# Cross-attention and an MX-FP8 feed-forward on one core: a new order of loads, a third place for queries and keys, two centerings on ScalarE

## The chip, the cores and the metric
One core of a Trainium2 chip runs the whole program in one launch. The metric is device microseconds of one execution; three executions of the kernel before gave 611.86 to 611.87 us, median 611.86. A profiled execution took 611.8 us by the same measure; its trace spans 610.0 us, so some 1.8 us lie around the trace.

## The reference
What is computed, cut to what matters (shapes: x 4x512x512, ctx 4x512x256, gate and up 2048x512, down 512x2048):

```python
x = x + xattn(layernorm(x), ctx, Wq, bq, Wk, bk)
x = x + ffn(layernorm(x), gate_w, up_w, down_w)

def xattn(logits, features, Wq, bq, Wk, bk):
    query = einsum('bnc,dc->bnd', features, Wq) + bq        # d = 128
    key = einsum('bnc,dc->bnd', features, Wk) + bk
    attention = softmax(einsum('bnd,bmd->bnm', query, key), axis=-1)
    return einsum('bln,bmn->blm', logits, attention)

def mx_dequant(t):     # blocks of 32 along the last dimension, e4m3
    scales = maximum(max_abs(blocks) / 448, 1e-30)
    return (blocks / scales).astype(float8_e4m3fn).astype(float32) * scales

def mx_linear(x, w):
    return mx_dequant(x) @ mx_dequant(w).T

def ffn(x, gate_w, up_w, down_w):
    h = silu(mx_linear(x, gate_w)) * mx_linear(x, up_w)
    return mx_linear(h, down_w)
```

## The kernel before
Everything stands in one function that writes an instruction list for each engine: SP (issues loads, stores and transposing DMAs), GpSimd (Pool: one reduction over partitions per weight unit, and accumulating DMAs), TensorE, ScalarE and VectorE. Each list is a row of calls of small helpers in an order written out by hand. An engine works its list strictly in order; between the lists stand only semaphores. So what sets the order around the change is these lists, and a table `bank_uses` that says, for each of the eight PSUM banks, which result uses it after which: a result waits until the one before it in its bank has been read (`take_bank`, `bank_left`).

Work is cut so:

- Attention, for each batch b of 4: `project(b, i)` makes the queries (i=0) and keys (i=1) from the context, `take_projection` copies them with the bias to SBUF; `energies(b, nt)` makes 128 rows of logits; `row_max` (VectorE), `exponential` (ScalarE) and `weigh` (ScalarE: identity times 1/sum) follow; `turn_probs(b, nt)` multiplies a piece of the exponentials by this diagonal, which turns and scales it; `take_probs` copies that to `AT`; `attend(b, lt)` multiplies the raw x columns by `AT`; `add_attended` (VectorE) adds it to the rows of x. These matmuls are float32. `row_means` and `row_variances` are the first layernorm's statistics on ScalarE.
- The 12 weight units (gate and up of four column groups, then four pieces of down), each 128x2048: load to one of three places `W`, then on VectorE `unit_reduce`, `unit_largest`, `unit_scale`, `unit_round`, `unit_dequant`, on ScalarE `unit_magnitude`, `unit_rescale`, then split into two float16 parts: `unit_hi` (ScalarE) writes the high part, an accumulating DMA of Pool (`unit_rest`) subtracts it from `W`, and `unit_lo` (ScalarE) writes what is left. SP turns each part with a transposing DMA (`turn_unit_hi`, `turn_unit_lo`).
- The rows of x after attention, batch by batch (`center`, `rows_scale`, `rows_round`, `rows_dequant`, `rows_hi`, `rows_rest`, `rows_lo`, `turn_rows_hi`, `turn_rows_lo`), the same way, into one of two places of `xT`. For batches named in `rows_by_vector` VectorE writes the low part without the DMA.
- `product(r, c)`: gate and up of 128 rows r (0 to 15) and 512 columns c: 24 matmuls of 512 columns in float16 (high by high, high by low, low by high). `silu_of` (ScalarE) and `hidden_of` (VectorE) make 128x512 of the hidden layer; a row's four pieces are quantized (`hidden_scale`, `hidden_round`, `hidden_dequant`), split (`hidden_hi`, `hidden_lo`) and turned into one of two places `hT`. The split's buffer has one place for each part: `hidden_lo(r)` waits until the low part of row r-1 has been turned, and `hidden_hi(r)` until `hidden_lo(r-1)` has read the high part. `turn_hidden_hi(r)` waits until `down(r-2)` is done.
- `down(r)`: 48 matmuls of 512 columns. `down_last` does row 15 in two halves of 48 matmuls of 256 columns; it starts when both parts of row 15 have been turned.
- TensorE begins with 18 matmuls of zeros (`keep_zeros`).

In the trace each line is that of a helper: L664 `project`, L671 `energies`, L678 `turn_probs`, L687 `attend`, L703 `product`, L715 and L718 `down`, L734 `down_last`, L748 `keep_zeros`, L929 `take_projection`, L970 `take_probs`, L1575 `hidden_lo` on VectorE, L1054 `hidden_hi`, L417 and L422 the turning of a hidden row's high and low part. A float32 matmul of the program stands as two in the trace.

Of the kernel before, what the change touches and what calls it, by code (L numbers as in the profile page):

```python
# [13 lines left out]
P = 128  # L14
# [18 lines left out]
def xattn_ffn(nc, xrows, xcols, ctxT, consts, units, out):  # L33
# [35 lines left out]
        ("p0.0 e1.0 p2.0 t1.1 e2.3 t2.3 a2.3 u1.0 u2.0 g6.1 g2.2 u5.1 g6.3 g1.3 u4.3 d0 u8.1 u9.3 g11.2 g14.1 g13.0"  # L69
         " g12.3 g10.2 u15.0 d8 d12").split(),  # L70
        ("p0.1 e1.1 a0.1 a0.3 e2.1 t2.1 a2.1 u3.0 g2.0 u6.0 u5.0 g5.2 u5.3 u1.2 g7.0 u7.3 g9.0 g10.0 u11.2 g14.2"
         " g13.1 g8.2 g10.3 g15.1 d7 d11").split(),
        ("p1.0 e1.2 a0.2 t1.3 a1.1 e3.1 t3.2 a3.0 g2.1 g4.1 g3.2 g0.2 u0.3 u3.3 g7.2 d1 u9.1 g11.0 d4 u12.1 u14.3"
         " u13.2 u8.3 u11.3 d6 d10").split(),
        ("p1.1 e1.3 e2.0 a1.2 e3.2 t3.3 a3.1 u2.1 g5.0 g5.1 u0.2 g1.2 u4.2 u7.2 u8.0 g9.3 g11.1 g12.1 g14.3 g13.2"
         " g8.3 g11.3 g15.2 d9").split(),
        ("e0.0 t0.0 p2.1 t1.2 a1.0 e3.0 t3.1 u0.0 u3.1 u4.0 u6.2 u0.1 g1.1 g4.2 u7.1 g8.0 g9.2 u11.0 g14.0 g12.2"
         " g13.3 g10.1 d5 g15.3 d15").split(),
        ("e0.1 t0.1 p3.0 a1.3 e3.3 g3.0 a3.2 g6.0 u4.1 u3.2 g5.3 u1.1 g4.3 g7.3 g8.1 u9.2 u11.1 u14.0 u12.2 u13.3"
         " u10.1 g15.0 u15.3").split(),  # L80
# [7 lines left out]
    rows_by_vector = (0,)  # L88
    logged = (0,)
    hidden_by_vector = (6, 7, 8, 9, 10, 11, 12, 13, 14, 15)  # L90

    with ExitStack() as stack:
# [42 lines left out]
        probs = [early[:, n * UNIT:(n + 1) * UNIT].rearrange("p (t n) -> p t n", n=512) for n in range(2)]  # L135
# [3 lines left out]
        qT, kT = late[:, 0:512], late[:, 512:1024]  # L139
# [1744 lines left out]
```

## Time and profile before

| what | us |
|---|---|
| median of three executions | 611.86 |
| profiled execution, by the same measure | 611.8 |
| span of its trace | 610.0 |
| TensorE busy | 602.0 (99%) |
| VectorE busy | 494.8 (81%) |
| ScalarE busy | 301.3 (49%) |
| GpSimd busy | 44.4 (7%) |

TensorE is busy in nearly the whole span, and the chain that ended last is TensorE in 93% of it. Busy time counts an instruction from its start to its end, so what matters for the time is when TensorE had nothing to start. The granted clock is at its upper level (2.4 GHz) in every slice, though the matmuls of zeros at the start run at half of that rate for the first 5 us.

### The profile page before, as it was taken

How to read it: one execution, taken by the hardware profiler on the slowest of the kernel's cores; microseconds unless marked ns; L12 is line 12 of the kernel's file. 1: busy time of each engine (PE TensorE's matmuls, PEld its weight loads, DVE VectorE, ACT ScalarE, POOL GpSimd, SP SyncE). 2: the span in 40 equal slices, each digit the busy share in tenths (PEclk: the TensorE clock that was granted, in tenths of full speed). 3: DMA queues.
4: the chain of work that ended last, by engine and by line, in shares of the span. 5: the costliest groups of instructions: out<-in, count | busy, mean ns of one | idle time of the engine just before them, and what ended most of it. 6: DMA issues, size and time to landing. Idle time of an engine off the chain costs nothing.

```text
span 610.0 us, 7226 instructions
## 1 busy us (share of the span) xinstructions
PE 602.0 (99%) x2690; PEld 282.8 (46%) x2690; DVE 494.8 (81%) x469; ACT 301.3 (49%) x449; POOL 44.4 (7%) x58
## 2 busy tenths in 40 slices
PE   8999999999999999999999999999999999999998
PEld 3545545444444444444444444444444444444446
DVE  6999999999999999995999999421149999899810
ACT  3699999536555554743656644411114233454420
POOL 0010002100000000011002101000000000010100
PEclk9999999999999999999999999999999999999999
DMA  8936999999888868987766768700000222775981
GB/s 317 414 118 168 224 240 258 254 236 227 186 199 198 224 139 167 234 151 155 156 140 132 134 137 167 120 1 0 2 1 0 45 43 40 133 124 102 153 141 34
DMA packets 147874, 90.18 MB, mean 148 GB/s; under 512 B 134272, under 2 KB 134656, under 8 KB 143232
## 3 DMA queue, kind: packets, MB, share of 16 engines
q1 hardware_dynamic: 142656, 63.78, 45.0%
q0 software_dynamic: 5184, 25.95, 19.1%
q8 instruction: 21, 0.34, 0.2%
q14 instruction: 13, 0.11, 0.1%
HBM read 25.76 MB, written 8.39 MB: 56 GB/s over the span
## 4 chain that ended last, share of the span: by engine, by line
PE 93%; DMA 3%; ACT 2%; SPq 0%; issue 0%; DVEq 0%; DVE 0%; POOLq 0%; ACTq 0%
PE bank L703 54%; PE bank L715 16%; PE bank L687 9%; PE bank L718 8%; PE bank L671 2%; PE bank L678 2%; PE bank L734 2%; DMA gu_hi<-in_ctxT 1%; DMA xT<-W 1%; DMA W<-W 1%; PE bank L664 1%; ACT h L943 0%; ACT h L934 0%; ACT W L1014 0%; ACT dn L970 0%
## 5 line engine op out<-in xcount | busy, mean ns | idle before, releaser
L703 PE MATMUL bank<-gu_hi,xT 128*128 128x512 f16 x1024 | 243.1, 379 | 0.4 <-DMA xT<-W 0.4
L703 PEld LDWEIGHTS bank<-gu_hi,xT 128*128 128x128 f16 x1024 | 100.0, 98 | 121.7 <-DMA xT<-W 1.2
L703 PE MATMUL bank<-gu_lo,xT 128*128 128x512 f16 x512 | 131.4, 379 | 0.0
L715 PE MATMUL bank<-dn,hT 128*128 128x512 f16 x480 | 106.0, 379 | 0.0
L1028 ACT ACTIVATE silu<-bank,unscale 128x512 f32<-128x512 f32 x64 | 43.2, 683 | 116.7 <-PE bank L703 72.0
L1543 DVE SCALAR_TENSOR_TENSOR h<-bank,unscale,silu 128x512 f32<-128x512 f32 x64 | 46.8, 747 | 60.4 <-PE bank L703 56.8
L703 PEld LDWEIGHTS bank<-gu_lo,xT 128*128 128x128 f16 x512 | 50.1, 98 | 60.4
L715 PEld LDWEIGHTS bank<-dn,hT 128*128 128x128 f16 x480 | 47.0, 98 | 56.6
L687 PE MATMUL bank<-dn,h 128*128 128x512 f32 x128 | 55.8, 592 | 0.0
L718 PE MATMUL bank<-dn,hT 128*128 128x512 f16 x240 | 54.2, 379 | 0.0
L1071 ACT ACTIVATE y<-bank,xnmr,odown 128x128 f32<-128x128 f32 x60 | 22.6, 457 | 55.0 <-PE bank L718 55.0
L1054 ACT ACTIVATE W<-h 128x2048 f16<-128x2048 f32 x16 | 30.5, 1909 | 25.2 <-DMA hT<-W 11.4
L898 ACT ACTIVATE mag<-h 128x2048 bf16<-128x2048 f32 x18 | 34.2, 1899 | 15.5 <-DVE h L1379 14.8
L1378 DVE SCALAR_TENSOR_TENSOR h<-mag,h 128x2048 f32<-128x2048 bf16 x18 | 41.2, 2287 | 0.8 <-ACT mag L898 0.8
L1379 DVE SCALAR_TENSOR_TENSOR h<-mag,h 128x2048 f32<-128x2048 bf16 x18 | 41.2, 2292 | 0.6
L687 PEld LDWEIGHTS bank<-dn,h 128*128 128x128 f32 x128 | 24.2, 190 | 29.8 <-issue 29.7
L1557 DVE TENSOR_TENSOR h<-h,rscale 128x2048 f32<-128x2048 f32 x16 | 36.7, 2292 | 0.5
L1569 DVE TENSOR_TENSOR h<-h,hscale 128x2048 f32<-128x2048 f32 x16 | 36.6, 2290 | 0.3
L1552 DVE TENSOR_REDUCE hscale<-h 128x64 f32<-128x2048 f32 x16 | 36.5, 2282 | 0.3
L718 PEld LDWEIGHTS bank<-dn,hT 128*128 128x128 f16 x240 | 23.5, 98 | 28.3
L1575 DVE SCALAR_TENSOR_TENSOR W<-h,W 128x2048 f16<-128x2048 f32 x10 | 22.9, 2290 | 15.6 <-DMA hT<-W 15.6
L1378 DVE SCALAR_TENSOR_TENSOR W<-mag,W 128x2048 f32<-128x2048 bf16 x14 | 32.0, 2286 | 1.9 <-ACT mag L898 1.9
(108 smaller groups left out, 557.2 us busy)
## 6 DMA issues: line engine op xcount, KB each, us to landing
W<-hT POOLq DMA_DIRECT2D x12, 1024.0 KB, 6.0
W<-in_units SPq DMA_DIRECT2D x11, 1024.0 KB, 5.9
h<-W POOLq DMA_DIRECT2D x6, 1024.0 KB, 5.8
h<-in_xcols SPq DMA_DIRECT2D x4, 1024.0 KB, 10.7
out_y<-y POOLq DMA_DIRECT2D x15, 256.0 KB, 4.9
h<-in_xrows SPq DMA_DIRECT2D x2, 1024.0 KB, 14.9
out_y<-h SPq DMA_DIRECT2D x2, 1024.0 KB, 11.1
W<-out_y SPq DMA_DIRECT2D x2, 1024.0 KB, 5.9
```

The source lines that it names most:

```text
L687: last = pe.matmul(bank[:, :], xTf[b % 2][:, j, lt * P:(lt + 1) * P], AT[:, j, :], start=(j == 0), stop=(j == HT - 1))
L703: last = pe.matmul(bank[:, :], xT[:, b % 2, part, k, :], w[:, c, g, j * 512:(j + 1) * 512], start=(j == 0 and not low), stop=(j == HT - 1 ...
L715: pe.matmul(bank[:, :], hT[:, r % 2, 0, k, :], dn[:, w, k, :], start=(k == 0 and w == 0), stop=False)
L718: last = pe.matmul(bank[:, :], hT[:, r % 2, 1, k, :], dn[:, 0, k, :], start=False, stop=(k == IT - 1))
L898: nc.scalar.activation(mag[:, :], v, ACT.Abs, scale=MAGIC).then_inc(mag_ready, 1)
L1028: nc.scalar.activation(silu[:, n % 2, :], bank_of(f"g{r}.{c}")[:, :], ACT.Silu, scale=unscale[:, 2 * c:2 * c + 1]).then_inc(silu_ready, 1)
L1378: then(dve.scalar_tensor_tensor(v, mag[:, :], floor, v, ALU.max, ALU.add))
L1379: dve.scalar_tensor_tensor(v, mag[:, :], floor, v, ALU.max, ALU.subtract).then_inc(mag_used, 1)
L1543: dve.scalar_tensor_tensor(hrow(r)[:, c * 512:(c + 1) * 512], bank_of(f"u{r}.{c}")[:, :], unscale[:, 2 * c + 1:2 * c + 2], silu[:, n % 2, ...
L1552: then(dve.tensor_reduce(s, blocks(row), AX.X, ALU.max, apply_absolute_value=True))
L1557: dve.tensor_tensor(blocks(row), blocks(row), each_block(rscale[:, :]), ALU.mult).then_inc(hv_ready, 1)
L1569: dve.tensor_tensor(blocks(row), blocks(row), each_block(hscale[:, r % 2, :]), ALU.mult).then_inc(hd_ready, 1)
```

## The change
What it does:

- SP loads the first context and the constants first, then the halves of the first weight unit, and has another order of the later loads, transposes and stores. `turn_rows_hi(0)` now stands behind a wait for the accumulating DMA of unit 2.
- Queries and keys have three places instead of one, exponentials and diagonals four instead of two.
- The low part of the rows of batch 0 is no longer written by VectorE but through the accumulating DMA and ScalarE; hidden row 6 likewise. Centering of batches 2 and 3 goes from VectorE to ScalarE.
- The lists of all engines and the bank table are written in another order. TensorE makes the energies of batch 0 right after its projections, spreads the last projections, energies and turns, takes `keep("a2.0", 4)` (four more 128x128 matmuls) ahead of the attention of batch 2, and near the end does `product(15, 3)` after `down(11)`.

The core of the diff (the ordered lists and the bank table in two lines of each):

```diff
-        ("p0.0 e1.0 p2.0 t1.1 e2.3 t2.3 a2.3 u1.0 u2.0 g6.1 g2.2 u5.1 g6.3 g1.3 u4.3 d0 u8.1 u9.3 g11.2 g14.1 g13.0"
...
+        ("p0.0 p2.0 t0.1 t0.3 a0.0 a0.3 e3.1 t3.1 u1.0 g3.1 u6.1 u2.2 u5.2 g0.3 u1.3 u7.0 u2.3 u9.0 g10.0 g11.1"
...
-    rows_by_vector = (0,)
+    rows_by_vector = ()
-    hidden_by_vector = (6, 7, 8, 9, 10, 11, 12, 13, 14, 15)
+    hidden_by_vector = (7, 8, 9, 10, 11, 12, 13, 14, 15)
...
-        probs = [early[:, n * UNIT:(n + 1) * UNIT].rearrange("p (t n) -> p t n", n=512) for n in range(2)]
+        lower = [gu_lo[:, c, :, :].rearrange("p g n -> p (g n)").bitcast(F32) for c in (1, 2)]
+        spare = xT[:, 1, :, :, :].rearrange("p a k n -> p (a k n)").bitcast(F32)
+        probs = [place.rearrange("p (t n) -> p t n", n=512)
+                 for place in (early[:, 0:UNIT], early[:, UNIT:2 * UNIT], *lower)]
-        qT, kT = late[:, 0:512], late[:, 512:1024]
+        qk = [(place[:, 0:512], place[:, 512:1024]) for place in (late, spare, spare[:, 1024:])]
...
+                if 2 <= u <= 5 and part == 1:
+                    sp.wait_ge(probs_turned, LT * (u // 2 + 2))
...
+                if b == 1:
+                    sp.wait_ge(energy_ready, LT * 3)
...
+            load_ctx(0)
+            load_consts()
             load_half(0)
             load_rest(0)
-            load_consts()
-            load_ctx(0)
             load_unit(1)
+            load_ctx(2)
             load_ctx(1)
...
             product(15, 2)
-            product(15, 3)
-            down(6)
-            down(7)
-            down(8)
             down(9)
             down(10)
             down(11)
+            product(15, 3)
             down(12)
...
-                if b > 0:
-                    act.wait_ge(energy_ready, LT * b)
+                if b >= 3:
+                    act.wait_ge(energy_ready, LT * (b - 2))
...
+            def center_by_scalar(b):
+                act.wait_ge(ymean_ready, b + 1)
...
+                src = X[b] if b < 2 else late_xw
+                for lt in range(LT):
+                    cols = slice(lt * H, (lt + 1) * H)
+                    last = nc.scalar.activation(xw_of(b)[:, cols], src[:, cols], ACT.Identity,
+                                                bias=nmean[:, LT * b + lt:LT * b + lt + 1])
+                last.then_inc(xnorm_ready[b], 1)
```

TensorE's list at its start, before. L664 is a projection (two matmuls each), L671 an energy, L678 a turn of exponentials (four each), L687 an attention (four each):

```order
L748 MATMUL bank<-dn 128x512 x18
L664 MATMUL bank<-gu_hi,gu_lo 128x512 x8
L671 MATMUL bank<-gu_lo 128x512 x8
L678 MATMUL bank<-h,dn 128x128 x16
L664 MATMUL bank<-h,gu_lo 128x512 x8
L687 MATMUL bank<-dn,h 128x512 x12
```

And now; the same helpers have the lines L669, L677, L684 and L693:

```order
L754 MATMUL bank<-dn 128x512 x18
L669 MATMUL bank<-gu_hi,gu_lo 128x512 x4
L677 MATMUL bank<-gu_lo 128x512 x4
L669 MATMUL bank<-gu_hi,gu_lo 128x512 x4
L669 MATMUL bank<-h,gu_lo 128x512 x4
L677 MATMUL bank<-xT 128x512 x2
L684 MATMUL bank<-h,dn 128x128 x4
L677 MATMUL bank<-xT 128x512
L669 MATMUL bank<-h,gu_lo 128x512 x2
L677 MATMUL bank<-xT 128x512
L684 MATMUL bank<-h,dn 128x128 x8
```

The energies of batch 0 moved up to right behind the first two projections, and the projections of batches 1 and 2 behind them.

SP's list where the first rows are turned, before (L381 and L386 turn the high and low part of a weight unit, L398 and L403 those of rows, L337 loads columns of x, L344 stores rows):

```order
L386 DMA_TRANSPOSE gu_lo<-hT 128x16x128 [waits wlo_ready,wrest_in]
L398 DMA_TRANSPOSE xT<-hT 128x16x128 [waits nhi_ready]
L403 DMA_TRANSPOSE xT<-hT 128x16x128 [waits nlo_made]
L381 DMA_TRANSPOSE gu_hi<-hT 128x16x128 [waits whi_ready]
L319 DMA W<-in_units 128x2048 [waits wlo_ready]
```

And now (L384, L389 units; L403, L408 rows; `wrest_in` is counted by the accumulating DMAs of the units):

```order
L384 DMA_TRANSPOSE gu_hi<-hT 128x16x128 [waits whi_ready,wrest_in]
L389 DMA_TRANSPOSE gu_lo<-hT 128x16x128 [waits wlo_ready]
L338 DMA h<-in_xcols 128x4x512 [waits attended]
L403 DMA_TRANSPOSE xT<-hT 128x16x128 [waits nhi_ready,wrest_in]
L408 DMA_TRANSPOSE xT<-hT 128x16x128 [waits nlo_ready]
L345 DMA out_y<-h 128x4x512 [waits x1_ready]
```

The rows' high part got a wait on `wrest_in`, and the low part is now made by ScalarE (`nlo_ready`) instead of VectorE (`nlo_made`).

VectorE's list at its end, before, from inside `hidden_scale(15)` on (L1393 and L1557 are in `hidden_scale`, L1378 and L1379 `hidden_round`, L1575 `hidden_lo`, L1569 `hidden_dequant`):

```order
L1393 RECIPROCAL rscale<-hscale 128x64 [waits hv_ready]
L1557 TENSOR_TENSOR h<-h,rscale 128x2048 [waits dve_step]
L1385 TENSOR_SCALAR hpow<-hmax 128x1
L1559 RECIPROCAL hrpow<-hpow 128x1 [waits dve_step]
L1378 SCALAR_TENSOR_TENSOR h<-mag,h 128x2048 [waits mag_ready,hv_ready]
L1379 SCALAR_TENSOR_TENSOR h<-mag,h 128x2048 [waits dve_step]
L1575 SCALAR_TENSOR_TENSOR W<-h,W 128x2048 [waits hT_in1,hhi_ready]
```

And now, the whole of what follows `hidden_of(15, 3)` from the same place on (L1415 and L1579 `hidden_scale(15)`; L1597 `hidden_lo(13)` and in the last row of 14 and 15; L1591 `hidden_dequant(14)`, then of 15; L1400 and L1401 `hidden_round(15)`):

```order
L1415 RECIPROCAL rscale<-hscale 128x64 [waits hv_ready]
L1579 TENSOR_TENSOR h<-h,rscale 128x2048 [waits dve_step]
L1407 TENSOR_SCALAR hpow<-hmax 128x1
L1581 RECIPROCAL hrpow<-hpow 128x1 [waits dve_step]
L1597 SCALAR_TENSOR_TENSOR W<-h,W 128x2048 [waits hT_in1,hhi_ready]
L1591 TENSOR_TENSOR h<-h,hscale 128x2048 [waits hdscale_ready,mag_used]
L1400 SCALAR_TENSOR_TENSOR h<-mag,h 128x2048 [waits mag_ready,hv_ready]
L1401 SCALAR_TENSOR_TENSOR h<-mag,h 128x2048 [waits dve_step]
L1591 TENSOR_TENSOR h<-h,hscale 128x2048 [waits hdscale_ready,mag_used]
L1597 SCALAR_TENSOR_TENSOR W<-h,W 128x2048 [waits hT_in1,hhi_ready] x2
```

`hidden_round(14)`, `hidden_lo(12)` moved ahead of the last piece of row 15, so that less stands behind it; but the piece itself comes from a `product(15, 3)` that TensorE now does three rows of `down` before its last row, where before ten rows of `down` stood between them.

## Rows read from the trace of the kernel before
**Rows 1.** The page: busy us (share of the span) xinstructions, by engine.
```profile
PE 602.0 (99%) x2690; PEld 282.8 (46%) x2690; DVE 494.8 (81%) x469; ACT 301.3 (49%) x449; POOL 44.4 (7%) x58
```
**Rows 2.** Waits of TensorE: who <- for whom: us in total, times, longest.
```profile
PE bank L671 <- ACT gu_lo L929: 1.5, 1, 1.5
PE bank L664 <- DMA gu_hi<-in_ctxT: 1.4, 1, 1.4
...
PE bank L664 <- ACT dn L970: 0.4, 1, 0.4
PE bank L703 <- DMA xT<-W: 0.4, 1, 0.4
```
**Rows 3.** Timeline 0 to 80 us: start, us, engine, line, operation [idle before <-releaser].
```profile
4.81 1.22 DVE L1479 TENSOR_REDUCE scale<-W 128x32 f32<-128x1024 f32 x1 [3.68 <-DMA W<-in_units]
...
6.67 0.75 PEld L748 LDWEIGHTS bank<-dn 128*128 128x128 f16 x4 [0.24 <-issue]
...
9.30 0.30 PEld L664 LDWEIGHTS bank<-gu_hi,gu_lo 128*128 128x128 f32 x2 [1.89 <-issue]
...
20.31 1.27 ACT L929 ACTIVATE gu_lo<-bank,gu_lo 128x512 f32<-128x512 f32 x2 [5.52 <-PE bank L671]
...
74.91 2.04 ACT L970 ACTIVATE dn<-bank 128x512 f32<-128x512 f32 x4
```
**Rows 4.** The chain that ended last, in order of time: start us, us, what.
```profile
57.27 13.73 PE bank L687 x32
71.01 3.57 PE bank L678 x32
74.58 3.44 PE bank L671 x8
78.01 13.73 PE bank L687 x32
...
95.32 15.54 PE bank L703 x72
...
289.75 6.11 DMA xT<-W
...
586.17 6.91 PE bank L715 x32
...
596.53 10.49 PE bank L734 x96
```
**Rows 5.** DMA issues by group: count, KB each, median us to landing.
```profile
W<-hT POOLq DMA_DIRECT2D x12, 1024.0 KB, 6.0
...
h<-hT POOLq DMA_DIRECT2D x1, 1024.0 KB, 9.6
```
**Rows 6.** VectorE's timeline, 160 to 585 us.
```profile
160.99 0.75 DVE L1543 SCALAR_TENSOR_TENSOR h<-bank,unscale,silu 128x512 f32<-128x512 f32 x1 [0.98 <-PE bank L703]
...
549.92 0.74 DVE L1543 SCALAR_TENSOR_TENSOR h<-bank,unscale,silu 128x512 f32<-128x512 f32 x1
...
556.43 2.29 DVE L1378 SCALAR_TENSOR_TENSOR h<-mag,h 128x2048 f32<-128x2048 bf16 x1
...
560.97 2.28 DVE L1575 SCALAR_TENSOR_TENSOR W<-h,W 128x2048 f16<-128x2048 f32 x1
...
584.73 2.29 DVE L1575 SCALAR_TENSOR_TENSOR W<-h,W 128x2048 f16<-128x2048 f32 x1 [6.65 <-DMA hT<-W]
```
**Rows 7.** The last transposes: SP's timeline, and a row of ScalarE's.
```profile
575.88 1.96 SPq L417 DMA_TRANSPOSE hT<-W  x1
578.11 4.71 SPq L422 DMA_TRANSPOSE hT<-W  x1
586.24 1.76 SPq L417 DMA_TRANSPOSE hT<-W  x1
588.10 2.24 SPq L422 DMA_TRANSPOSE hT<-W  x1
...
580.41 1.91 ACT L1054 ACTIVATE W<-h 128x2048 f16<-128x2048 f32 x1 [3.06 <-DMA hT<-W]
```

More of the change, by code:

```diff
@@ L1143, in _ @@
             take_probs(2, 3)
-            unit_rescale(3)
-            unit_magnitude(3)
-            unit_lo(1)
-            rows_hi(0)
             exponential(3, 0)
+            unit_hi(2)
             exponential(3, 1)
@@ L1255, in _ @@
-            silu_of(8, 0)
-            hidden_magnitude(3)
-            silu_of(8, 1)
-            hidden_hi(2)
-            hidden_lo(2)
-            hidden_unscale(4)
-            hidden_magnitude(4)
+            silu_of(2, 3)
+            rows_hi(2)
+            rows_lo(2)
+            hidden_rescale(2)
+            hidden_magnitude(2)
+            hidden_magnitude(3)
+            silu_of(8, 0)
+            hidden_hi(2)
+            silu_of(8, 1)
+            center_by_scalar(3)
+            take_down(0)
@@ L1269, in _ @@
             hidden_lo(3)
-            rows_magnitude(3)
-            silu_of(10, 0)
-            hidden_hi(4)
-            take_down(2)
-            rows_hi(3)
-            hidden_lo(4)
-            silu_of(11, 0)
-            hidden_unscale(5)
             hidden_rescale(5)
             hidden_magnitude(5)
-            hidden_rescale(6)
-            hidden_unscale(6)
-            hidden_magnitude(6)
-            rows_lo(3)
-            hidden_hi(5)
-            take_down(3)
-            add_constant()
@@ L1287, in _ @@
-            hidden_unscale(7)
+            hidden_lo(4)
+            rows_hi(3)
+            silu_of(10, 0)
+            rows_lo(3)
+            take_down(2)
+            hidden_hi(5)
+            hidden_magnitude(6)
+            hidden_rescale(6)
+            silu_of(11, 0)
+            hidden_magnitude(7)
             hidden_rescale(7)
-            hidden_magnitude(7)
+            hidden_lo(5)
+            hidden_unscale(3)
             silu_of(11, 1)
-            take_down(4)
-            hidden_lo(5)
+            silu_of(11, 2)
@@ L1334, in _ @@
[L1334 to L1349 removed]
+            hidden_magnitude(9)
@@ L1655, in _ @@
+            row_max(3, 1)
+            add_attended(1, 2)
+            add_attended(1, 3)
+            unit_dequant(2)
+            unit_reduce(3)
+            row_max(3, 2)
+            unit_largest(3)
+            row_max(3, 3)
+            unit_scale(3)
+            unit_reduce(4)
+            attended_means(1)
+            unit_largest(4)
+            center(1)
+            row_sum(3)
+            rows_scale(1)
+            add_attended(2, 0)
+            unit_power(3)
             unit_round(3)
```

666 lines of the change are left out of this document (329 added, 337 removed).

## The prediction
> **What bounds the kernel now.** First the page's busy times: TensorE is busy in 602.0 of 610.0 us [rows 1], so only the moments in which it has nothing to start can be won, and any wait added to it is paid whole. Second its waits: 1.4 us for the first context, 1.5 us for the queries and keys of batch 1, 0.4 us for a bank, 0.4 us for the turned rows of batch 2 [rows 2]. Third the chain of waits, which gives the prices at full speed: a product (24 matmuls) is 15.54/3 = 5.18 us, a `down` 596.53 - 586.17 = 10.36, one `attend` 13.73/4 = 3.43, one `turn_probs` 3.57/4 = 0.89, one `energies` 3.44/4 = 0.86 [rows 4]; one `project`, four float32 matmuls of the trace at the rate of the attention (13.73/32 = 0.43), is 1.72. The change adds no matmul work but `keep`, so the sum is a list of waits, at their places.
>
> **Start, -1.7 us.** The last weights of the zeros are loaded by 7.4, and the first real weights at 9.30, when context 0 has landed [rows 3]. It was the fifth load; the first one (0.5 MB) had landed by 4.81, when VectorE starts on it [rows 3]. With the context first and the constants second, both should be there by 7.6, and TensorE starts there. Bounds: -1.9 (nothing waits) and -0.9 (the constants' two loads are late by 0.8).
>
> **Waits of the attention, -0.9.** From 9.30 to the first `attend` of batch 1 at 57.27 lie 47.97 us [rows 3, 4]. In it: 8 `project`, 12 `energies`, 8 `turn_probs`, 4 `attend`, 13.76 + 10.32 + 7.12 + 13.73 = 44.93. So TensorE lost 3.0 us there. In the new order it first waits for the queries and keys of batch 0 (a copy is 0.64 [rows 3], with the drain 1.1), then has energies and two batches of projections to do while ScalarE makes the exponentials, and loses 1.0 at `turn_probs(0, 3)`, whose diagonal stands behind `row_means(0)`, `row_variances(0)` and a 1.8 us copy in ScalarE's list. The separate places take away the waits for old queries. I count 2.1. Bounds: 1.5 and 3.5, so -1.5 to +0.5.
>
> **The attention of batch 2, +1.2.** By 20.31 ScalarE had not begun to copy batch 1's keys [rows 3]; in the new list it has by then these two copies and four exponentials done, about 4 us ahead. Ahead of `take_probs(2, 3)` it has two 1.8 us copies more (`unit_lo(1)`, `rows_hi(0)`), and that instruction also needs `turn_probs(2, 3)`, which TensorE ends near 75.5. It ended by 76.95 before [rows 3] and I expect 76.5 now. `attend(2, 0)` started at 78.01 [rows 4]; without a wait it would start at 78.0 - 2.6 = 75.4, so 1.1 to 1.2 are lost, in which the four matmuls of `keep` (0.9) lie hidden. If ScalarE is quicker, `keep` still costs its 0.9; if it is later by 1, it is 2.2.
>
> **Product (3, 0), +0.6.** Before, it ran at 95.32 [rows 4]; now TensorE asks for it at 92.1 (1.4 earlier, and two turns, 1.8, behind it). It needs the rows of batch 0 turned. SP now turns them behind the accumulating DMA of unit 2, which can be issued only when ScalarE has done `unit_hi(2)`, behind `take_probs(2, 3)` and an exponential: 76.5 + 0.7 + 1.8 = 79.0. Such a DMA lands in 6.0, or in 9.6 where another runs beside it, and `rows_rest(0)` does, from 75 on [rows 5]: 85.1 to 87. A transpose lands in 4.5 (575.88 to 580.41), one issued 2.2 behind it at 584.73, 4.3 after the first [rows 7, 6]. High part 90 to 91.5, low part 92.6 to 96; the product needs the low part 8 matmuls in, at 93.8. So 0 to 2.2, I take 0.6. The rows' low part itself goes from VectorE (2.29) to a DMA and a copy; that chain (75 + 6.5 + 1.8 = 83.3) is under the wait for unit 2, so it costs nothing while that wait is there.
>
> **Product (6, 0), +0.3.** `rows_lo(1)` stands on ScalarE behind `unit_magnitude(5)`, which needs `unit_scale(5)`, which stands on VectorE behind the last `add_attended(3, 3)`. From the end of the attention of batch 3: 0.9 + 2.8 + 1.9 + 1.8 + 4.6 of transposing = 12.0; the product needs it after two products and 8 matmuls, 10.36 + 1.73 = 12.1. Bounds 0 and 1.5 (a transpose of rows took 6.11 when a second followed [rows 4]).
>
> **Middle, -0.35.** The 0.4 at the rows of batch 2 (landing 289.75 + 6.11 = 295.86 [rows 4]) goes if VectorE keeps ahead; around 161 it waited 0.98 for TensorE [rows 6], so it follows TensorE's shift, and it has less to do (centering of batches 2 and 3, 1.7 each; a low part, 2.29) until then. Bounds -0.35 and +1. `down` of rows 2 to 4 now comes 13 to 18 us earlier; by my count the low part of row 3 lands at 344 and is needed at 349, so this costs nothing; with 5 us lost it would cost all above that.
>
> **End, +1.5.** Before, `down_last` started on time: row 15's parts were turned from 586.24 on, when `down(13)` was over, and landed by 596.5 [rows 7, 4]. Now, counted from the end of `product(15, 3)`: TensorE wants the last row after three `down`, at 31.1. VectorE needs 0.1 + 6.5 (last piece and `hidden_scale`, 549.92 to 556.43) + 2.2 (`hidden_lo(13)`) + 2.2 (dequantize row 14) + 4.55 (round, 556.43 to 560.97, with the step between) + 2.2 + 2.2 (`hidden_lo(14)`) = 20.0 [rows 6]. The transpose of row 14's low part lands at 24.6; only then may `hidden_lo(15)` write, until 26.9. Row 15's high part is issued at 22.0. Where transposes follow each other 4.3 apart, as in rows 7, they land at 28.9 and 33.2: a wait of 2.2. Where the queue is free, the last one lands at 26.9 + 4.5 = 31.4: 0.3. I take 1.5, nearer to the only pair that shows it. VectorE's own arrears don't add: by the same prices it is done with `hidden_of(15, 2)` some 5 us before the last piece. The other side of it: `product(15, 3)` behind `down(11)` lets rows 8 to 11 be multiplied while VectorE works on the later ones; that hides nothing that TensorE waited for before.
>
> The Trainium skill (DMA: Bandwidth & Descriptors, section Latency and other measured facts) gives 261 GB/s for a DMA transpose. By that, our 0.5 MB would hold the queue for 2.0 us, an estimate from that page; the trace disagrees for this pair, where the second landed 4.3 after the first. With 2.0 the end would wait 0.3 and product (3, 0) nothing, 1.8 less in all than my sum.
>
> **Sum.** -1.7 - 0.9 + 1.2 + 0.6 + 0.3 - 0.35 + 1.5 = +0.65. The profiled execution took 611.8 (span 610.0), 0.06 below the median: 612.4, against 611.86. The other lists (order of units, `take_down`, `add_constant`, the odd `hidden_unscale`) cost nothing as long as TensorE has a bank and operands, which I found for each product with 2 us or more to spare.
>
> **Rivals.**
> A, faster: transposes follow each other closely and the rows of batch 0 are in time. For it: `down_last` after 588.10 waited for nothing, and a fourth transpose in a row need not take longer than one. Terms: -1.7 - 0.9 + 1.2 - 0.35 + 0.3 = -1.45: 610.4. With `keep` alone (0.9) paid in batch 2, 610.1.
> B, slower, one mechanism: transposes queue behind each other at 4.3 us or more. It acts where SP issues the rows of batch 0 (low part at 96: +2.2), at product (6, 0) (+0.8) and at the end (+2.2): -1.75 + 5.2 = +3.45: 615.3; with the end alone at 2.2 and the rest as I took it, 613.1. It decides from where the last low part lands later than 31.1 after `product(15, 3)`. For it: the pair at 575.88 and 578.11. Against it: the pair at 586.24 and 588.10 had landed by 596.5.
> C: the start brings nothing, because the constants' two loads, not the context, end the wait: +1.5: 613.5. Against it: they were issued ahead of the context and are small. I count it with the slower ones.
>
> **Chances.** About 0.2%, 1.2 us, is what a measurement of this kernel can tell from no change. The forecast with what lies near it, 610.7 to 613.1: 0.38, its own range. A: 0.32. B and C: 0.30 (0.24 and 0.06). The range that leaves out 2 in 10 is 609.8 to 615.4, from A with nothing lost at batch 2 to B.
>
> **What would show it.** The first weights of a projection at 7.5 to 7.8, and 9.3 would refute the first term. `attend` of batch 1 at 56.4 or so, of batch 2 at 76.5. In TensorE's waits a new line of a product for the DMA into `xT` near 92 to 96, and one of `down_last` for the DMA into `hT` near the end; no such line there and the end term is wrong. Any TensorE wait over 1 us between 150 and 550 would show a list that I thought covered.

## The result and the profile after

The changed kernel takes 613.27 us (median of 9 executions, 611.27 to 614.85), the kernel before 611.87 in the same comparison (611.60 to 611.97): a ratio of 1.0023 by the medians, with a 95% interval of 1.0012 to 1.0029. It is slower by 1.4 us. The profiled execution took 613.43 with a span of 611.6, against 610.0 for the span before. I forecast 612.4. The median lies 0.2 above the stretch that I had put around the forecast (610.7 to 613.1) and inside the wide range (609.8 to 615.4); the terms of the sum were partly wrong.

The waits of TensorE in the changed kernel answer to [rows 2]. Columns: who <- for whom: us in total, times, longest.

```profile
PE bank L740 <- DMA hT<-W: 2.3, 1, 2.3
PE bank L754 <- DVE dn L1612: 1.2, 1, 1.2
PE bank L684 <- ACT h L965: 1.0, 1, 1.0
PE bank L677 <- ACT gu_lo L935: 0.8, 1, 0.8
PE bank L709 <- DMA xT<-hT: 0.4, 1, 0.4
```

The two waits for contexts and for batch 1's keys are gone, and the largest wait now stands at the very end: `down_last` (L740) for the turned low part of row 15. TensorE's timeline of the same kernel shows where it stands at each step (start us, us, engine, line, operation, idle before <- releaser); the rows are to be held against [rows 3, 4].

```profile
7.50 3.60 PE L669 MATMUL bank<-gu_hi,gu_lo 128*128 128x512 f32 x8
...
32.41 1.13 PE L684 MATMUL bank<-h,dn 128*128 128x128 f32 x8 [0.97 <-ACT h L965]
...
56.83 10.54 PE L693 MATMUL bank<-dn,h 128*128 128x512 f32 x24
...
75.93 1.06 PE L748 MATMUL bank<-gu_lo 128*128 128x128 f32 x8
76.93 13.97 PE L693 MATMUL bank<-dn,h 128*128 128x512 f32 x32
...
92.52 1.03 PE L709 MATMUL bank<-gu_hi,xT 128*128 128x512 f16 x4
...
141.42 1.90 PE L709 MATMUL bank<-gu_hi,xT 128*128 128x512 f16 x8 [0.41 <-DMA xT<-hT]
...
592.09 3.62 PE L724 MATMUL bank<-dn,hT 128*128 128x512 f16 x16
598.04 10.64 PE L740 MATMUL bank<-dn,hT 128*128 128x256 f16 x96 [2.33 <-DMA hT<-W]
```

The first projection starts at 7.50, the attention of batch 2 at 76.93, where the four matmuls of `keep` fill the gap ahead of it, and product (3, 0) starts at 92.52 with no wait. Held against the same work in the kernel before, TensorE is ahead by 0.3 to 2.0 up to the last `down`; the last row is behind by 1.7.

The end, in the timelines of VectorE and SyncE of the changed kernel, answers to [rows 6, 7]. L1597 is `hidden_lo`, L427 and L422 start the transposes of a low and a high part; for SPq rows the second number is how long the issue held SyncE.

```profile
564.77 0.75 DVE L1565 SCALAR_TENSOR_TENSOR h<-bank,unscale,silu 128x512 f32<-128x512 f32 x1 [5.10 <-PE bank L709]
...
582.57 2.28 DVE L1597 SCALAR_TENSOR_TENSOR W<-h,W 128x2048 f16<-128x2048 f32 x1
584.88 1.84 SPq L427 DMA_TRANSPOSE hT<-W  x1
586.90 3.79 SPq L422 DMA_TRANSPOSE hT<-W  x1
591.30 2.29 DVE L1597 SCALAR_TENSOR_TENSOR W<-h,W 128x2048 f16<-128x2048 f32 x1 [6.45 <-DMA hT<-W]
593.62 1.32 SPq L427 DMA_TRANSPOSE hT<-W  x1
```

The last piece of row 15 comes right behind `product(15, 3)`, 20.1 us later the low part of row 14 is ready, but its transpose lands only 6.4 us after its issue. The last low part is written behind that, and lands at 598.0.

### The profile page after: what moved, and what is told of

Same layout as the page of the kernel before. It is cut to its first block, busy times and chain, and to the rows that moved or that the text cites. A ratio compares the mean times of both kernels' runs of the same rounds, so it can differ in the third digit from the quotient of the medians.

```text
span 611.6 us, 7228 instructions
## 1 busy us (share of the span) xinstructions
PE 603.0 (99%) x2698; PEld 283.9 (46%) x2698; DVE 485.4 (79%) x459; ACT 306.9 (50%) x459; POOL 50.4 (8%) x60
## 4 chain that ended last, share of the span: by engine, by line
PE 81%; DMA 5%; ACT 5%; DVE 5%; issue 3%; POOL 0%; SPq 0%; DVEq 0%; POOLq 0%; ACTq 0%
PE bank L709 49%; PE bank L721 14%; PE bank L693 7%; PE bank L724 7%; PE bank L740 2%; DMA hT<-W 2%; PE bank L684 1%; DMA W<-hT 1%; DMA W<-in_units 1%; PE bank L677 1%; ACT hT L923 1%; DVE W L1597 1%; DMA xT<-hT 1%; ACT mag L905 1%; ACT h L949 0%
## 5 line engine op out<-in xcount | busy, mean ns | idle before, releaser
L693 PE MATMUL bank<-dn,h 128*128 128x512 f32 x128 | 55.9, 593 | 0.0
L1400 DVE SCALAR_TENSOR_TENSOR h<-mag,h 128x2048 f32<-128x2048 bf16 x18 | 41.2, 2287 | 7.8 <-ACT mag L905 7.8
L905 ACT ACTIVATE mag<-h 128x2048 bf16<-128x2048 f32 x18 | 34.3, 1904 | 25.9 <-DVE h L1401 16.3
L1401 DVE SCALAR_TENSOR_TENSOR h<-mag,h 128x2048 f32<-128x2048 bf16 x18 | 41.3, 2292 | 0.6
L693 PEld LDWEIGHTS bank<-dn,h 128*128 128x128 f32 x128 | 24.1, 190 | 29.7 <-issue 28.7
L1579 DVE TENSOR_TENSOR h<-h,rscale 128x2048 f32<-128x2048 f32 x16 | 36.7, 2292 | 0.5
L1591 DVE TENSOR_TENSOR h<-h,hscale 128x2048 f32<-128x2048 f32 x16 | 36.6, 2287 | 0.2
L905 ACT ACTIVATE mag<-W 128x2048 bf16<-128x2048 f32 x14 | 26.7, 1907 | 20.0 <-DVE W L1522 10.6
L1400 DVE SCALAR_TENSOR_TENSOR W<-mag,W 128x2048 f32<-128x2048 bf16 x14 | 32.0, 2285 | 3.1 <-ACT mag L905 3.0
L1597 DVE SCALAR_TENSOR_TENSOR W<-h,W 128x2048 f16<-128x2048 f32 x9 | 20.6, 2288 | 15.6 <-DMA hT<-W 15.6
```

The source lines that it names most:

```text
L693: last = pe.matmul(bank[:, :], xTf[b % 2][:, j, lt * P:(lt + 1) * P], AT[:, j, :], start=(j == 0), stop=(j == HT - 1))
L905: nc.scalar.activation(mag[:, :], v, ACT.Abs, scale=MAGIC).then_inc(mag_ready, 1)
L1400: then(dve.scalar_tensor_tensor(v, mag[:, :], floor, v, ALU.max, ALU.add))
L1401: dve.scalar_tensor_tensor(v, mag[:, :], floor, v, ALU.max, ALU.subtract).then_inc(mag_used, 1)
L1579: dve.tensor_tensor(blocks(row), blocks(row), each_block(rscale[:, :]), ALU.mult).then_inc(hv_ready, 1)
L1591: dve.tensor_tensor(blocks(row), blocks(row), each_block(hscale[:, r % 2, :]), ALU.mult).then_inc(hd_ready, 1)
```

## The experiments

Each ratio is to the kernel before, from runs on the same chip. "The down(10) version" is the changed kernel with one line moved, as in experiment 2.

**Experiment 1: the changed kernel again,** to see how far two measurements of it differ.

> The changed kernel unaltered, as the yardstick of this chip. Theory A (the end waits for row 15's last transposes, which come late because product(15, 3) is late): a wait of down_last for the DMA into hT of 2 to 2.6 us in the profile again, median near 613.3, and its spread (3.6 us in nine runs, against 0.4 before) comes from the landing of these transposes. Theory B (what varies is some wait earlier in the program): the end's wait is the same in a run of another time, and another TensorE wait differs.

615.06 (612.56 to 615.73, 6 runs), 1.0049 [1.0035, 1.0062]. The waits were the same, with 0.8 more for the constants at the start. The profiled execution took 615.54, with a span 2.1 longer than the first. By product (3, 1) it is 0.5 behind; most of the rest arises at one place. TensorE's timeline and two windows of it (window, its length, busy us and count of PE, PEld, DVE, ACT and POOL, then granted clock, DMA share, GB/s):

```profile
598.47 12.31 PE L740 MATMUL bank<-dn,hT 128*128 128x256 f16 x96 [2.31 <-DMA hT<-W]
```

```profile
594.00:598.00 4.00, 2.16 (x11) 0.78 (x8) 0.02 (x1) 1.50 (x4) 0.00 (x0) 1.00 0.70 131
598.00:602.00 4.00, 3.53 (x19) 2.58 (x20) 0.00 (x0) 0.00 (x0) 0.89 (x1) 0.62 0.51 66
```

The granted clock was 0.62 from 598 to 602, that is at 1.2 instead of 2.4 GHz for much of it, right behind the wait, and the last row took 12.31 instead of 10.64. So the end wait can cost 1.7 on top of its 2.3. Theory A had the wait (2.3) but not the median (615.06 for 613.3), and neither theory had the clock.

**Experiment 2: `product(15, 3)` behind `down(10)`,** so one `down` (10.36) more lies between the last product and the last row.

```diff
             down(10)
+            product(15, 3)
             down(11)
-            product(15, 3)
             down(12)
```

> Only product(15, 3) moved one down forward, behind down(10) instead of down(11); the lists of the other engines unchanged. Theory A: VectorE loses its 5.1 us wait for that product, row 15 is ready 5 us sooner, down_last no longer waits (0 to 0.3 us): 2.3 us less than the changed kernel, 611.0, below the kernel before by 0.8, and the spread falls under 1 us. Theory B (the transposes are late by themselves, at 4.3 to 6.3 us each and beside the output's accumulating DMA): the wait stays above 1.5 us and the time near 613.

610.86 (610.20 to 612.62, 11 runs), 0.9987 [0.9978, 0.9995]: faster than both kernels. TensorE's waits in its profile:

```profile
PE bank L754 <- DVE dn L1612: 1.2, 1, 1.2
PE bank L677 <- ACT gu_lo L935: 0.8, 1, 0.8
PE bank L684 <- ACT h L965: 0.6, 1, 0.6
```

The wait of the last row is gone, and nothing came in its place. The end of the list alone made the change a loss. The spread did not fall under 1 us as theory A said: it is 2.4.

**Experiments 3 and 4: the order of the first loads,** taken back in the changed kernel, and put alone into the kernel before.

```diff
-            load_ctx(0)
-            load_consts()
             load_half(0)
             load_rest(0)
+            load_consts()
+            load_ctx(0)
```

> The changed kernel with the first four loads in the old order: halves of unit 0, then constants, then context 0. Theory A (the start is worth its 1.8 us): first projection at 9.3 instead of 7.5, and since ScalarE's list hangs on it, all of that stays: plus 1.5 to 1.9 us against the changed kernel, 615.1. Theory B (the wait for ScalarE at the attention of batch 2, 76.9, is set by VectorE's early units, which get their data 2.5 us sooner): the loss is made good there, plus 0 to 0.5 us.

614.21 (612.76 to 616.27, 6 runs), 1.0044 [1.0028, 1.0060]. The first projection is back at 9.19, attention of batch 2 at 78.02, product (3, 1) at 129.85 (+1.1 against the changed kernel), and the end wait is 2.4. By the profile the old order costs 1.1, between theory A (1.5 to 1.9) and theory B (0 to 0.5); the median is not told apart from experiment 1 by so few scattered runs.

> The kernel before with nothing but the new order of the first four loads. Theory A (that order pays only with the new lists): ScalarE's old list copies the keys of batch 0 behind unit_magnitude(0), and unit 0 is 2.5 us later; energies start near 17.6 instead of 16.2: 1 to 1.4 us slower than before, 613.0. Theory B (the load order is the whole gain of the start): 1.4 to 1.8 us faster than before, 610.2.

614.11 (612.87 to 615.48, 6 runs), 1.0042 [1.0030, 1.0054]: alone, the new order of loads makes the kernel before slower by 2.4. Its TensorE rows:

```profile
7.62 3.60 PE L664 MATMUL bank<-gu_hi,gu_lo 128*128 128x512 f32 x8
14.01 3.70 PE L664 MATMUL bank<-gu_hi,gu_lo 128*128 128x512 f32 x8 [2.80 <-DMA gu_hi<-in_ctxT]
```

It starts 1.7 earlier and then waits 2.8 for context 1, which now lands later, so its energies start at 17.56 instead of 16.61, where theory A had them. A second wait lies under this one: ScalarE copies the keys of batch 0 behind `unit_magnitude(0)`, which now waits for unit 0 and starts at 14.69 instead of 11.98, so the keys were there only at 17.5. With 0.7 more lost behind ScalarE, the profile is 1.9 longer, more than the 1 to 1.4 of theory A. The new TensorE list has the energies of batch 0 at that place (11.87 to 15.6), and with it the new order of loads gains some 0.5 (experiment 10).

**Experiment 5: ten matmuls of row 14 again into the last row's bank,** in the end wait.

```diff
                 bank = take_bank(f"d{r}")
+                for k in range(10):
+                    pe.matmul(bank[:, :], hT[:, (r - 1) % 2, 0, k, :], dn[:, 0, k, :], start=True, stop=True)
                 pe.wait_ge(hT_in[0], 16 * (r + 1))
```

> The changed kernel with ten matmuls of 128x512 (2.2 us) of row 14 put into the bank of the last row ahead of its wait, so that TensorE is busy while it waits; nothing reads their result. The changed kernel's own runs lay between 611.3 and 615.7, the kernel before between 611.5 and 612.1; in one profiled run of the changed kernel the granted clock was 0.62 from 598 to 602, behind the wait of 2.3, and the last row took 12.3 instead of 10.6. Theory D: the 2.3 us wait itself is the loss, and in some executions the clock falls behind it, 1.7 more. Then the wait becomes 0.1 to 0.3, the last row 10.6 in the profile, the median falls to 612.0 to 613.5 and no run is over 614. Rival E: the clock does not hang on this wait, and the spread comes from elsewhere (the start, say): runs up to 615 or more as before, median 613 to 615.

613.18 (611.87 to 614.42, 11 runs), 1.0019 [1.0011, 1.0028]. The last row starts at 597.54 without a wait of its own and takes 10.64. No run is as long as the slowest of the changed kernel (615.73), but one of 11 is above the 614 that I wrote, and the spread of 2.5 is no smaller than that of experiment 2.

The mean granted clock of every execution is on record and says how often the clock fell. In the kernels with the end wait (the changed kernel, experiments 3, 6 and 11) it is 0.996 or 0.997 in 13 of 32 executions, which took 614.0 to 616.3, and 0.999 or 1.000 in the other 19, which took 611.3 to 614.2. With the wait filled it is never below 0.999 (11 executions), and neither is it in the down(10) version and its variants (65 executions of 609.5 to 612.6) or in the kernel before (77). So the fall comes with the end wait; it explains the longest runs and not the whole scatter. Experiment 4, which has no end wait in its profile, shows 0.997 in 2 of 6 executions; its 2.8 us wait near 14 may be the place, but no profile caught one.

This profile also shows another end than I looked for:

```profile
584.72 1.81 SPq L427 DMA_TRANSPOSE hT<-W  x1
586.74 2.35 SPq L422 DMA_TRANSPOSE hT<-W  x1
589.30 2.29 DVE L1599 SCALAR_TENSOR_TENSOR W<-h,W 128x2048 f16<-128x2048 f32 x1 [4.61 <-DMA hT<-W]
```

The same two transposes, issued 2.02 apart as in the changed kernel, and yet row 14's low part was there after 4.6, not 6.4, and the second issue held SyncE for 2.35, not 3.79. The last low part was issued at 591.62 and was in near 596.0, an estimate from the 4.4 that it took in the changed kernel. So in this execution the last row would have waited about 0.6, and the ten matmuls, which end at 597.5, held it longer than the transpose did.

**Experiment 6: row 15's high part is turned only when row 14's low part has landed.**

```diff
             def turn_hidden_hi(r):
+                if r == RT - 1:
+                    sp.wait_ge(hT_in[1], 16 * r)
```

> The changed kernel, only SyncE starts the last high part's transpose when the low part of row 14 has landed, not 2 us after that one was issued. Theory A (two transposes that run together lengthen the first one: 6.3 for the low part of row 14, against 4.3 for one alone): that low part lands 4.4 after its issue at about 584.9, VectorE starts the last low part 1.9 earlier, at 589.4, and its transpose is issued at 591.7 beside the high part's; both are in by 596 to 596.7, the wait of the last row falls from 2.3 to 0.3 to 1.0, and the time by 1.3 to 2.0, more where the clock had fallen behind the wait. Rival B (they queue, 4.3 each, whatever the order): the low part of row 14 lands at 589.2, the high part at 593.5, the last at 597.8: the wait stays at 2.1 to 2.3, the time the same.

614.04 (612.46 to 615.15, 7 runs), 1.0031 [1.0021, 1.0042]; TensorE's last wait was 2.1. Its timelines of SyncE and VectorE:

```profile
584.45 1.81 SPq L429 DMA_TRANSPOSE hT<-W  x1
588.74 4.03 SPq L424 DMA_TRANSPOSE hT<-W  x1
588.82 2.29 DVE L1599 SCALAR_TENSOR_TENSOR W<-h,W 128x2048 f16<-128x2048 f32 x1 [4.40 <-DMA hT<-W]
592.86 1.35 SPq L429 DMA_TRANSPOSE hT<-W  x1
```

Both theories were half right. Alone, row 14's low part landed in 4.3, as A said. But the issue of the high part then held SyncE for 4.03, so the last low part, ready at 591.1, was issued at 592.86, and the wait stayed as B said. In these two profiles the second of two close transposes costs 2 us either in the first one's landing or in SyncE's next issue. In experiment 5 it did neither in full, so this is no fixed price.

**Experiment 11: the adds of rows 12 and 13 nearly empty,** to see whether GpSimd's DMA holds that transpose back.

```diff
-                nc.gpsimd.dma_start(out_rows[r], y[:, r % 2, :], accum_op=ALU.add).then_inc(out_added[r % 2], 16)
+                n = 2 if r in (12, 13) else H
+                nc.gpsimd.dma_start(out_rows[r][:, 0:n], y[:, r % 2, 0:n], accum_op=ALU.add).then_inc(out_added[r % 2], 16)
```

> The changed kernel, only the two accumulating DMAs that add rows 12 and 13 to the output, issued by GpSimd at 580.1 and 588.8, move 2 of their 512 columns (the other columns of these rows are left unadded). In the changed kernel the transpose of row 14's low part, issued at 584.9, was waited for until 591.2, and the DMA engines moved nothing from 589.5 to 591. Theory F: the adding DMA holds the landing back. Then row 14's low part lands 4.2 to 4.6 after its issue, VectorE starts the last low part at 589.3 to 589.6, the last row waits 0.3 or less, time 611 to 612. Theory G: the next transpose, issued 2.0 behind the first with an issue that holds SyncE for 3.8, holds it back, and the adds have no part in it: it lands 6.2 to 6.5 after its issue, the wait of the last row stays 2.1 to 2.4, time 612.5 to 615.

614.52 (613.23 to 615.64, 4 runs), 1.0043 [1.0030, 1.0056]. The timeline of SyncE, VectorE and TensorE, and a window, with columns as above:

```profile
585.48 1.84 SPq L427 DMA_TRANSPOSE hT<-W  x1
587.50 3.87 SPq L422 DMA_TRANSPOSE hT<-W  x1
591.96 2.29 DVE L1598 SCALAR_TENSOR_TENSOR W<-h,W 128x2048 f16<-128x2048 f32 x1 [6.51 <-DMA hT<-W]
...
598.68 12.21 PE L741 MATMUL bank<-dn,hT 128*128 128x256 f16 x96 [2.36 <-DMA hT<-W]
```

```profile
598.00:602.00 4.00, 3.32 (x17) 2.41 (x18) 0.00 (x0) 0.00 (x0) 0.89 (x1) 0.57 0.51 66
```

The first transpose landed 6.4 after its issue again, so theory F is out: the size of the adds has no part in it. Theory G's numbers all came (6.4, a wait of 2.4, 614.5), but its cause is only half of it, since experiment 5 has the same pair 2.0 apart and a landing of 4.6. In the profiles with the long landing (the changed kernel and experiments 1, 3 and 11) the second issue held SyncE for 3.8 to 3.9, in experiment 5 for 2.35; what decides between the two is open. And the clock fell behind the wait a second time (0.57, last row 12.21). Of the five profiled executions that had this wait, two had the fall and took 615.5 and 615.6; the three without took 612.8 to 614.2.

**Experiment 7: the down(10) version without `keep("a2.0", 4)`.**

```diff
-            keep("a2.0", 4)
```

> The changed kernel with its last product behind down(10), and without the four matmuls that are put in ahead of the attention of batch 2. With them that version took 610.86, span 608.6, its attention of batch 2 started at 76.7 to 76.8. My theory: these matmuls lie in a wait for the probabilities, so the attention of batch 2 starts at 76.7 again (within 0.2), with 0.9 more of waiting in front; time 610.4 to 611.3. Rival: TensorE was what the attention waited for, and it starts 0.4 to 0.9 earlier: 610.0 to 610.4. Second rival: they keep the clock up, and without them the granted clock falls below 1 between 77 and 90, which costs 1 to 2: 612 to 613.

610.69 (609.73 to 611.76, 11 runs), 0.9983 [0.9975, 0.9992]. The attention of batch 2 starts at 76.91, with a wait of 0.84 for the probabilities in front, as in my theory. The matmuls of `keep` lie hidden, and their absence does not bring the clock down. In this profile a wait of 1.15 for a diagonal of batch 3 came behind that attention; the executions don't show a price for it.

**Experiment 8: the down(10) version with batches 2 and 3 centred by VectorE.**

```diff
-            center_by_scalar(2)
...
-            center_by_scalar(3)
...
             attended_means(2)
+            center(2)
             hidden_of(4, 2)
...
             hidden_of(8, 1)
+            center(3)
             hidden_scale(4)
```

> The changed kernel with its last product behind down(10), and with batches 2 and 3 centred by VectorE as in the kernel before (1.7 us each on VectorE, 1.8 less each on ScalarE). My theory: between 142 and 550 TensorE never waits for either engine by less than 1 us, so the time is that of the version with ScalarE, 610.3 to 611.4, and no new wait of TensorE is over 0.3. Rival: VectorE is the nearer limit (37.5 of 38 us busy from 142 to 180), and its 1.7 us come back as a wait of TensorE for a bank or for the rows of batch 2 of 0.4 to 1.7: 611.3 to 612.6.

611.06 (11 of 12 runs from 609.55 to 611.89), 0.9984 [0.9975, 0.9992]: the same as with ScalarE. No new wait came between 142 and the end (that of product (6, 0), just before, is 0.7 here, as in experiment 11). VectorE's work in the middle is off the path.

**Experiments 9 and 10: the down(10) version again, and the same with the old first loads** (edit as in experiment 3).

> The changed kernel with its last product behind down(10), unaltered from the earlier run (610.86, 0.9987 of the kernel before), as the reference for the other runs of this call and to see whether it beats both kernels again. Expected 610.2 to 611.4, no wait of the last row, and a spread of about 2 as before, against 0.8 for the kernel before.

611.49 (609.93 to 612.05 for 11 of 12 runs), 0.9989 [0.9980, 0.9997]. It beats the kernel before again, by 0.3 here and 0.8 in experiment 2, at the upper edge of what I expected. The changed kernel itself didn't run beside it; elsewhere it took 613.27 and 615.06. TensorE waited 1.3 for context 1 here (0 in experiment 2).

> The changed kernel with its last product behind down(10) and the first four loads in the old order (half a unit of weights first, context 0 fifth). It tells two things apart. Price of the load order: theory, the first projection starts at 9.2 instead of 7.5 to 8.0, but the attention of batch 2 hangs on ScalarE, so of the 1.7 about 1.0 to 1.3 arrive there (77.8 to 78.1 instead of 76.7) and in the time: 611.6 to 612.2. Rival: the 1.7 arrive whole: 612.3 to 612.6; or nothing does: 610.9. Spread: if the new load order makes the runs scatter, this one scatters by less than 1; if something else in the change does, it scatters by 2 as the others.

611.94 (median of 10 runs from 611.51 to 612.51), 1.0001 [0.9993, 1.0010]. Two more of the twelve took 1,659 and 1,986 us, the profiled one among them, so its timeline is of no use here; the comparison leaves them out. So the new load order gains about 0.5 by the medians (611.94 against 611.43 for the 11 runs of experiment 9), less than the 1.0 to 1.3 that I wrote. The new lists with the old loads are no faster than the kernel before, and the new loads with the old lists are slower (experiment 4): the two edits need each other. And the scatter falls from 2.1 to 1.0: much of it comes with the new load order.

**Experiment 12: the fourth diagonal of batch 0 ahead of the copy of unit 0,** in the down(10) version.

```diff
             take_probs(0, 0)
+            weigh(0, 3)
             unit_hi(0)
             take_probs(0, 1)
-            weigh(0, 3)
```

> The changed kernel with its last product behind down(10), and on ScalarE the fourth diagonal of batch 0 (0.4) ahead of the 1.8 us copy for unit 0 instead of two places behind it. Theory: TensorE's wait of 0.6 to 1.0 for that diagonal near 32 goes, the attention of batch 0 starts 0.6 to 1.0 earlier (34.8 to 35.2), and since ScalarE had 0.4 of waiting for TensorE near 56, half of it or more arrives at the attention of batch 2 (76.1 to 76.5 instead of 76.7) and in the time: 610.1 to 610.6. Rival: ScalarE has no room, the gain turns into a wait of the same size ahead of the attention of batch 1 or 2 (76.7 again): 610.8, as without this edit. Second rival: the copy for unit 0, 0.4 later, delays its transpose and the later loads: product (3, 1) starts at 128.9 or later, 611.2.

610.96 (610.19 to 612.53, 11 runs), 0.9987 [0.9979, 0.9996]: not told apart from experiments 2 and 9. The wait was not for the diagonal alone:

```profile
31.93 1.16 PE L684 MATMUL bank<-h,dn 128*128 128x128 f32 x8 [0.90 <-ACT dn L972]
```

The releaser is now `take_probs(0, 1)` (L972), which empties the bank that `turn_probs(0, 3)` uses, and it stands behind the same copy: two waits lay on top of each other, and the profile named the later one. The first rival had the outcome (76.5 and 610.8, ScalarE has no room), though the wait stayed where it was. The rows below show why ScalarE has none.

**Where the start's gain went, and part of the scatter.** The experiments show where TensorE's early start was lost, at an engine that none of my terms priced. In the new order of loads unit 0 comes third, and ScalarE's list has `unit_magnitude(0)` (L905) behind the first two copies and ahead of all exponentials. Unit 0's first half was there by 9.12 in the changed kernel (VectorE starts on it then), by 4.81 before [rows 3], and ScalarE, which had no wait there before and started at 11.98, waits 3.08 and starts at 14.90:

```profile
9.12 1.22 DVE L1501 TENSOR_REDUCE scale<-W 128x32 f32<-128x1024 f32 x1 [7.99 <-DMA W<-in_units]
...
14.90 1.91 ACT L905 ACTIVATE mag<-W 128x2048 bf16<-128x2048 f32 x1 [3.08 <-DVE W L1522]
```

From there to the attention of batch 2 ScalarE waits three times in the changed kernel, 1.4 us in all, and the distance is the same in every profile with the new loads, whatever the first projection and context 1 did:

| profiled execution | first projection | context 1 | `unit_magnitude(0)` | attention of batch 2 | distance of the last two |
|---|---|---|---|---|---|
| changed kernel | 7.50 | 15.61 | 14.90 | 76.93 | 62.03 |
| experiment 1 | 7.91 | 16.14 | 15.45 | 77.47 | 62.02 |
| experiment 2 | 7.97 | 15.89 | 14.71 | 76.73 | 62.02 |
| experiment 5 | 7.45 | 15.86 | 15.17 | 77.19 | 62.02 |
| experiment 6 | 7.77 | 15.68 | 14.57 | 76.58 | 62.01 |
| experiment 7 (no `keep`) | 7.18 | 15.64 | 14.89 | 76.91 | 62.02 |
| experiment 8 | 7.49 | 15.88 | 15.20 | 77.22 | 62.02 |
| experiment 9 | 6.69 | 16.07 | 15.40 | 77.43 | 62.03 |
| experiment 11 | 6.75 | 15.91 | 15.24 | 77.27 | 62.03 |
| experiment 12 | 6.44 | 15.21 | 14.53 | 76.49 | 61.96 |

Context 1 is late too in most of them (TensorE waits 1.3 for it in experiment 9), but that wait only takes the place of a later one for ScalarE: experiments 2 and 5 have context 1 at 15.89 and 15.86 and the attention of batch 2 0.46 apart, as far as their `unit_magnitude(0)`. In experiment 3, with the old loads, `unit_magnitude(0)` started at 13.49 without a wait and the attention of batch 2 at 78.02, 68.8 behind the first projection: there the first projection was the limit. So the new order trades one limit for another, and the landing of unit 0 moves the attention of batch 2 by 1.0 between the earliest and the latest of these profiles. No run moved unit 0 alone.

## Why the prediction was right, and where it was not

The terms, read from the timelines of both kernels at the same work:

| term | forecast | measured | from |
|---|---|---|---|
| Start | -1.7 | -1.84 | 9.34 to 7.50 |
| Waits of the attention | -0.9 | -0.16 | attend(1,0) at 56.83 for 57.11, with two energies (1.72) more done |
| The attention of batch 2 | +1.2 | +1.08 | 76.93 for 77.85 |
| Product (3, 0) | +0.6 | 0 | no wait |
| Product (6, 0) | +0.3 | +0.6 | wait of 0.41 and its restart |
| Middle | -0.35 | -0.5 | the 0.4 of [rows 2] is gone |
| End | +1.5 | +2.5 | 598.04 for 596.36, from 0.81 ahead |

They sum to +1.7, the difference of the spans is 1.6; I had forecast +0.65. That the error is not larger is in part luck: the end and the waits of the attention came out 1.7 worse than I wrote, and product (3, 0) 0.6 better.

**End, the term that was mis-sized.** The mechanism was right and experiment 2 shows it: without the wait the change is a gain. VectorE's 20.0 us from the end of `product(15, 3)` came out as 20.2 (564.6 to 584.88), and the last landing at 33.4, which is where I had put it (33.2) for transposes 4.3 apart. I then took 1.5 between the two ends; the pessimistic end, 2.2, was the true one. The way there was another, so that the two ways meet in one number is luck: not the last transposes queued, but the first of the pair was late (6.4 where I had 4.6), and VectorE could write the last low part only behind it. Experiment 6 shows why the sum is the same: taken apart, the delay goes into SyncE's issue. Why the first was late is open: in experiment 5 the same pair gave 4.6, and the last low part was in at about 31.5, the optimistic end that I had priced (31.4).

**Waits of the attention, wrong by 0.7.** I counted 2.1 us lost between the first projection and batch 1's attention; 2.7 were. The waits that I had priced are there (0.9 and 1.2 with their restarts, for 1.1 and 1.0). What I put at nothing, without a reason, is unit 0: with the contexts and constants ahead of it, ScalarE idles 3.1 for it, and all that ScalarE does for the attention comes later. Where unit 0 came soonest after the first projection (experiments 2 and 6) the loss is 2.0 and 2.1, as I had it. The same cause keeps the start's gain from arriving whole: start, waits and batch 2 together were to give -1.4 and gave -0.92, and experiment 10 prices the load order at some 0.5 in the time. Another 0.2 of the 0.7 is my base: I read 9.30 and 57.27 from two different views, and TensorE's timeline of the kernel before alone gives 9.34 and 57.11, a loss of 2.8 and not 3.0.

**The attention of batch 2** came as forecast (76.93 for 76.5, 20.1 behind batch 1's start both times). The 0.4 between is the late unit 0 again (an estimate): at the distance of experiment 3 (68.8 behind the first projection) it would have been 76.3. That `keep` lies hidden is shown by experiment 7.

**Product (3, 0), wrong and harmless.** The rows' high part was issued at 85.41, at the early end of my 85.1 to 87, and the low part 1.8 behind it; the product needed both at 94.2 and had them. I took a middle value where both transposes could land in time.

**Product (6, 0)** had its wait, twice the size that I took in this profile and 0 to 0.7 in the others. **Middle** was right: no wait of TensorE between 142 and the last row, and experiment 8 shows that 1.7 us twice on VectorE are not on the path.

**The rivals.** A had the end and the rows of batch 0 in time: wrong for the end, right for the rows. B, transposes that cost 4.3 each in a row, had the size right at the end only, and not the way there; with "the end alone at 2.2" it gave 613.1, the nearest number on record to the measured 613.27. C, no gain from the start because of the constants, is wrong: the first projection started at 7.50, and the constants ended the wait by 0.8 in experiment 1 only. Its price was wrong too: without the start my sum is +2.35, 614.2, not 613.5. What it warned of came for another cause, since little of the start's gain reached the time. What none of them had is the fall of the granted clock behind the end wait, 1.6 to 1.7 us in the two profiles that caught it, and seen in the mean clock of 13 of 32 executions; it moves a median of few runs.

**Transfer and landing of a transpose.** Each slice of this view of experiment 6 (570 to 600 us, GB/s moved) is 0.75 us:

```profile
GB/s 110 0 0 0 0 24 215 217 208 92 123 169 154 205 214 169 27 180 98 0 23 215 217 210 56 0 82 126 204 193 289 156 175 216 212 95 0 0 82 109
```

Row 14's low part, issued at 584.45, is the stretch 23, 215, 217, 210, 56: some 0.5 MB in 2.5 to 3 us, and it landed 4.3 after its issue. The Trainium skill (DMA: Bandwidth & Descriptors, section Latency and other measured facts) gives 261 GB/s; the 215 of this row are 18% below that. My sentence that the trace disagrees took the landing for the transfer. What stands here between them, about 1.5 us, was in neither number.

## What to carry to other kernels

Where an engine that is busy all the time gets its last operands through a chain of other engines and transfers, count that chain from the piece that starts it, and leave it a whole unit of the engine's work as room: moving one product ahead of one `down` was worth 2.4 to 4.2 us by the medians, more than all the rest of the change. A load that is moved ahead makes others late, so price the landing of each load that it passes, and ask which engine waits for it: here the early context helped TensorE by 1.8 us and made ScalarE wait 3.1 for its first weights. And when a wait goes, look for a second one under it, since the profile names only the one that ended last.

## What the runs showed of the hardware that was not expected

- A transpose of 0.5 MB in 16 bits landed 4.3 us after its issue alone (experiment 6). With a second issued 2.0 behind it, it landed after 6.4 to 6.5 in four profiles (the changed kernel, experiments 1, 3 and 11) and after 4.6 in one (experiment 5). One issue held SyncE from 1.32 to 4.03 us at the end of these kernels; what sets it is left open.
- A wait of 2.3 us of TensorE was followed by a granted clock of 0.57 to 0.62 over the next 4 us in two of five profiled executions, and by 1.00 in three. By the mean clock of each execution, 13 of 32 with this wait had the fall, and none of the 153 without a wait of this size (experiment 5, the down(10) versions, the kernel before).
- Single executions of versions with `product(15, 3)` behind `down(10)` took 634, 1,659, 1,986 and 2,284 us (4 of 69). The first may be another matter: its mean granted clock was 0.949, that of the other three 1.00. In the one profile of such an execution (1,986 us) TensorE has no wait over 1.2, ScalarE's and VectorE's instructions keep their length, and TensorE's matmuls take 2.8 to 3.8 times as long while the granted clock reads 1.00. The attention of batch 0, 13.73 elsewhere:

```profile
115.39 52.51 PE bank L693 x32
```

Of the 77 executions of the kernel before that were made on the same chips beside these, none had this, and none of the changed kernel's. Whether it comes from the kernels or from chance is not settled.
